# A three-layer transformer block: rotary pair swap on VectorE instead of TensorE, row sums and gates as column tiles of 32, halved TensorE steps, a new order of steps

## The reference

```python
x = x + xattn(layernorm(x), ctx, ctx, mask)   # scores without softmax, 16 heads of 16, then layernorm
x = x + attn(layernorm(x))                    # causal softmax attention, 16 heads of 16
x = x + ffn(layernorm(x))                     # rotary attention, rmsnorm, shared SwiGLU + 8 experts, rmsnorm
```

```python
r = jnp.stack([x1 * cos - x2 * sin, x1 * sin + x2 * cos], axis=-1)
q, k = src @ Wq, src @ Wk_c @ Wk              # both roped; v = src @ Wv_c @ Wv
g = softmax(flat @ Wg_gate + group_bias)      # 2 groups; the best group's 4 experts, top 2 of them
out = x + silu_glu(flat, W_shared_in) @ W_shared_out + sum_e w[:, e] * (h @ W2_experts[e])
```

## Time and profile before

| | |
|---|---|
| median of three runs | 241.22 us (241.12 to 241.95) |
| span of the profiled execution, its own time | 239.0 us, first to last instruction |
| TensorE busy | 228.0 us (95%) in 2304 matmuls |
| VectorE busy | 171.9 us (72%) |
| ScalarE busy | 121.4 us (51%) |
| POOL busy | 75.3 us (32%) |
| moved by DMA | 26.35 MB |
| first Gram matmul, last matmul's end | 6.0 us, 234.2 us |

### The profile page before, as it was taken

The page is one execution under the profiler, slowest core; times in us unless marked ns, Lnnn a source line. Parts: engine busy times, 40 slices in busy tenths (PEclk is TensorE's granted clock), DMA queues, the critical chain, the costliest instruction groups (busy, mean ns, idle before and its releaser), DMA issues.

```text
span 239.0 us, 5721 instructions
## 1 busy us (share of the span) xinstructions
PE 228.0 (95%) x2304; PEld 205.4 (86%) x2304; DVE 171.9 (72%) x370; ACT 121.4 (51%) x245; POOL 75.3 (32%) x89
## 2 busy tenths in 40 slices
PE   6989899999999999999999999999999999999991
PEld 6987797999999889978989999988878879998881
DVE  0757876966987879887966789586697764448353
ACT  3754575238571766386177977815451553550000
POOL 3011026222634020513549567745110020731011
PEclk9999999999999999999999999999999999999998
DMA  6899999828153452023304511100000000000001
GB/s 221 265 298 394 353 357 320 300 85 268 75 175 102 106 174 71 21 69 109 88 4 118 170 70 32 58 1 3 0 3 0 3 0 3 0 22 3 3 0 66
DMA packets 9434, 26.35 MB, mean 110 GB/s; under 512 B 1464, under 2 KB 2752, under 8 KB 9280
## 3 DMA queue, kind: packets, MB, share of 16 engines
q1 hardware_dynamic: 9120, 25.47, 32.4%
q10 hardware_dynamic: 288, 0.52, 0.6%
HBM read 25.46 MB, written 0.52 MB: 109 GB/s over the span
## 4 chain that ended last, share of the span: by engine, by line
PE 83%; DMA 7%; issue 3%; ACT 3%; DVE 2%; SPq 1%; POOLq 0%; POOL 0%; DVEq 0%
PE ps L704 77%; DMA raw<-in_ctx 7%; PE ps L707 5%; ACT ch L578 1%; DVE cl L1143 1%; ACT probT L511 1%; SPq L403 0%; DVE Z L1304 0%; SPq L358 0%; POOLq L363 0%; POOL rstd L463 0%; ACT z0T L511 0%; DVE X L1313 0%; DVE mb L1184 0%; DVE xHL L1273 0%
## 5 line engine op out<-in xcount | busy, mean ns | idle before, releaser
L704 PE MATMUL ps<-ch 128*128 128x130 f32 (+1 forms) x208 | 51.4, 264 | 1.5 <-DVE cl L1143 1.4
L704 PE MATMUL ps<-ch,cl 128*128 128x260 f32 (+1 forms) x208 | 51.1, 308 | 0.0
L704 PE MATMUL ps<-w,hT 128*128 128x512 f32 (+1 forms) x204 | 45.9, 382 | 0.0
L704 PEld LDWEIGHTS ps<-w,hT 128*128 128x128 f32 x204 | 36.4, 188 | 7.7 <-issue 0.7
L1143 DVE TENSOR_TENSOR cl<-raw,ch 128x1024 fp32r<-128x1024 f32 (+4 forms) x31 | 31.9, 1051 | 14.9 <-ACT ch L578 14.7
L704 PEld LDWEIGHTS ps<-ch 128*128 128x128 f32 (+1 forms) x208 | 39.5, 190 | 2.9 <-issue 1.4
L704 PEld LDWEIGHTS ps<-ch,cl 128*128 128x128 f32 (+1 forms) x208 | 39.2, 188 | 0.2
L463 POOL TENSOR_TENSOR rstd<-ve,half_exp 128x1 f32<-128x1 f32 (+1 forms) x22 | 13.8, 628 | 73.0 <-DVE ve L1022 72.9
L578 ACT ACTIVATE ch<-raw 128x1024 fp32r<-128x1024 f32 (+4 forms) x31 | 27.5, 916 | 12.9 <-DMA raw<-in_ctx 10.8
L704 PE MATMUL ps<-xHL,dense 128*128 128x256 f32 x192 | 24.3, 285 | 0.0
L704 PEld LDWEIGHTS ps<-xHL,dense 128*128 128x128 f32 x192 | 23.4, 192 | 0.2
(11 more groups left out here) (161 smaller groups left out, 417.7 us busy)
## 6 DMA issues: line engine op xcount, KB each, us to landing
raw<-in_ctx SPq DMA_DIRECT2D x22, 512.0 KB, 4.6
raw<-in_w SPq DMA_DIRECT2D x8, 512.0 KB, 3.8
stage<-in_dense SPq DMA_DIRECT2D x4, 512.0 KB, 5.9
w<-in_w SPq DMA_DIRECT2D x4, 256.0 KB, 6.9
w<-in_w SPq DMA_DIRECT2D x1, 1024.0 KB, 8.4
mask<-in_mask SPq DMA_DIRECT2D x1, 800.5 KB, 7.5
raw<-in_ctx SPq DMA_DIRECT2D x8, 65.0 KB
raw<-in_ctx ACTq DMA_DIRECT2D x2, 256.0 KB, 4.7
```

Of the source, the lines that this page charges most:

```text
L704: return pe.matmul(o, l, r, start=start, stop=stop, skip_group_check=not check)
```

## The change

The shuffle, the column tiles and the halves, cut to the lines that matter:

```diff
 # rotary: VectorE, step keys2 (rotate and roped are gone, also on POOL, ScalarE, TensorE)
-                    for swapped, (dst, by) in enumerate(((kcos, "cos"), (krot, "sin"))):
-                        last = dve.tensor_tensor(dst[i % 2][:, :, :], ...
-                    last.then_inc(own("k_parts", i), 1)
+                    both = ps[:, tile_bank(i):tile_bank(i) + 2, 0:D]
+                    link(dve.stream_shuffle(turned.rearrange("p b c n -> p b (c n)"), both, SWAP))
+                    dve.tensor_tensor(summed, both..., const("cos")..., ALU.mult).then_inc(own("qk_taken", i), 1)
+                    link(dve.tensor_tensor(turned, turned, const("sin")..., ALU.mult))
+                    dve.tensor_tensor(summed, summed, turned, ALU.add).then_inc(own("roped", i), 1)
 # rotary: TensorE, step keys2 (values2 has no TensorE part any more)
-                    for swapped in range(2):
-                        for ob in range(KC):
-                            last = mm(ps[:, tile_bank(i), swapped * D + ob * P:swapped * D + (ob + 1) * P],
-                                      wkv[0:P // 2, swapped, ob * P:(ob + 1) * P], kvcT[i % 2][0:P // 2, :], True, True)
+                    for ob in range(KC):
+                        last = mm(ps[:, tile_bank(i), ob * P:(ob + 1) * P], wkv[0:P // 2, ob * P:(ob + 1) * P],
+                                  kvcT[i % 2][0:P // 2, :], True, True)
+                        if ob == 0:
+                            mm(ps[:, tile_bank(i) + 1, D:2 * D], kvcT[i % 2][P // 2:P, :], wkv[P // 2:P, :], True, True)
 # rotary: ScalarE (no copy to qs; values2 waits for qk_taken; keys_roped writes qp and kblk)
-                    act.wait_ge(own("q2", i), i // 2 + 1)
-                    copy(qs[i % 2][:, :, :], ps[:, tile_bank(i) + 1, 0:D]...)
 # row sums, TensorE: from cross2_product to cross3; svn on VectorE and its product on POOL move along
-                                last = mm(ps[:, CROSS_B[0], jb * 2:(jb + 1) * 2], w0[:, 2, k, jb * P:(jb + 1) * P],
-                                          scol[:, k, i - 1:i + 1], k == 0, k == KC - 1)
+                                for r in range(P // PAIR):
+                                    mm(ps[r * PAIR:(r + 1) * PAIR, CROSS_B[0], jb * 2:(jb + 1) * 2],
+                                       w0[:, 2, k, jb * P + r * PAIR:jb * P + (r + 1) * PAIR], scol[:, k, i - 1:i + 1],
+                                       k == 0, k == KC - 1)
 # gates, TensorE
+                            for r in range(P // PAIR):
+                                mine = slice(r * PAIR, (r + 1) * PAIR)
+                                last = mm(ps[mine, tile_bank(1) + 1, t * 16:t * 16 + GRP + E],
+                                          xT[:, k, t * P + r * PAIR:t * P + (r + 1) * PAIR], gate[:, k, :], ...)
 # halves, TensorE: each pair is the old step cut in two
+                elif step in ("gram_rows", "gram"):
+                elif step in ("cross2_half", "cross2_product"):
+                elif step in ("hidden_half", "hidden_product"):
+                elif step in ("experts_half", "experts_product"):
```

More of the change, by code:

```diff
@@ L74, in constants @@
     return c
+SWAP = [lane ^ 1 for lane in range(32)]
 NU = 5 + 8
@@ L117, in second_half_steps @@
     return [
[L118 to L122, removed]
@@ L123, in second_half_steps @@
-        ("gram", 19), ("roped", 0), ("shares", (1, 0)), ("score_product", (0, 1)), ("split", 21), ("score", (0, 1)),
-        ("turn_p", (1, 0)), ("cross1", 5), ("piece", 3), ("exp", (0, 1)), ("gram", 20), ("values", (1, 0)),
-        ("evac", 6), ("cross2_product", 5), ("shares", (0, 1)), ("cross2", 5), ("project", (1, 0)),
-        ("turn_p", (0, 1)), ("norm2", 1), ("cross3", 5), ("norm2_end", 1), ("split", 22), ("values", (0, 1)),
-        ("cross4", 5), ("turn_z", (1, 1)), ("project", (0, 1)), ("split", 23), ("proj2_product", 1), ("rotate", 1),
@@ L128, in second_half_steps @@
-        ("square", 0), ("rms1", 0), ("roped", 1), ("keys2", 1), ("values2", 1), ("keys_roped", 1), ("rms1_end", 0),
-        ("cross1", 6), ("gram", 21), ("turn_x", 0), ("score_product", (1, 1)), ("piece", 4), ("xo_product", 2),
-        ("score", (1, 1)), ("xo", 2), ("exp", (1, 1)), ("cross2_product", 6), ("shares", (1, 1)), ("gram", 22),
-        ("gram", 23), ("cross2", 6), ("xo_end", 2), ("turn_p", (1, 1)), ("norm1", 2), ("evac", 7), ("cross3", 6),
[3 rows of a table removed]
-        ("values1", 2), ("turn_x", 1), ("cross4", 7), ("piece", 8), ("score_product", (2, 0)), ("score", (2, 0)),
@@ L156, in second_half_steps @@
-        ("experts", (1, 2)), ("experts", (1, 3)),
+        ("turn_z", (0, 1)), ("norm1", 1), ("cross2", 4), ("cross2_product", 4), ("gram_rows", 17), ("norm1_end", 1),
+        ("split", 18), ("split", 19), ("proj2_product", 0), ("gram", 17), ("evac", 5), ("turn_z", (1, 0)),
+        ("cross3", 4), ("keys2", 0), ("split", 20), ("proj1_product", 1), ("cross1", 5), ("queries", 1),
+        ("score", (1, 0)), ("score", (0, 1)), ("shares", (1, 0)), ("shares", (0, 1)), ("keys1", 1), ("values1", 1),
@@ new lines, in second_half_steps @@
+        ("split", 23), ("square", 0), ("gram_rows", 21), ("rms1_end", 0), ("turn_z", (1, 1)), ("cross4", 5),
+        ("cross1", 6), ("proj2_product", 1), ("turn_x", 0), ("keys2", 1), ("cross2_half", 6), ("cross2_product", 6),
+        ("xo_product", 2), ("gram", 21), ("gram_rows", 22), ("values2", 1), ("xo", 2), ("xo_end", 2),
+        ("score_product", (1, 1)), ("gram", 22), ("gram_rows", 23), ("gram", 23), ("keys_roped", 1), ("norm1", 2),
+        ("score", (1, 1)), ("cross2", 6), ("norm1_end", 2), ("cross3", 6), ("shares", (1, 1)), ("exp", (1, 1)),
@@ L481, in _ @@
                     last.then_inc(sem("gpre"), 1)
-                elif step == "cross2" and i % 2:
+                elif step == "cross3" and i % 2:
                     t = i // 2
@@ L791, in _ @@
                         pe.wait_ge(sem("mb"), i)
+                    if i > 1 and i % 2 == 0:
+                        pe.wait_ge(sem("svn"), i // 2)
                     bank = ps[:, CROSS_B[0], :]
```

298 lines of the change are left out of this document (145 added, 153 removed), and 6 rows, old and new, of the table USES.

## The result

The changed kernel takes 248.2 us (248.0 to 248.8) against 241.2: a ratio of 1.028, with a 95% interval of [1.026, 1.031]. A fourth execution took 253.4 us at a granted clock of 0.966, where the others had 0.985 to 0.993, and such slower executions are left out of every time and ratio here. The kernel is slower by 7.0 us, and lies 12.6 us above the forecast of 235.6 and outside the range. Its profiled execution has a span of 246.2 us.

A forecast was written before the change was run, and what follows sets the result against it. The prediction took the kernel as TensorE-bound from 6 to 234 us and summed -4.1 - 2.0 - 1.0 + 0.8 - 1.8 + 2.5 = -5.6 us, 241.22 to 235.6 us, range 230.8 to 239.6 (the forecast's own 232.5 to 238.5).

The forecast's parts named there:

- (b): Row sums `sv` on TensorE: column tiles of 32 in place of full-width products, four calls, -2.0 us.
- (c): Gates on TensorE in column tiles of 32, 0.95 us to 0.46, twice: -1.0 us.
- the slow rival: Rotary shuffle on VectorE is dear: from 2.3 us each it eats the 5.6 us gain; chance 0.07.
- (a): Rotary pair swap moved from TensorE to a VectorE shuffle: -4.1 us, bounds a gain of 3.6 to 4.6.
- (d): Larger steps halved: more re-entries of fp32r blocks behind fp32 steps on TensorE, +0.8 us (0 to 1.7).
- (f): New order behind the opening: old waits go, -1.6, new short hand-offs cost +4.1; together +2.5 us, bounds -1.6 and +5.
- (e): New order in the opening: TensorE's waits for the first Gram block and z0T shrink, -1.8 us, at most 2.9.
- The third rival: VectorE sets the pace up to 130 us, so only the part behind gains: 0.0 in all, 241.2 us; chance 0.14.
- the sign that I had set for being wrong: TensorE's idle time between 44 and 130 us grows by more than 5 us, or the shuffle takes over 1.5 us.

The follow-up runs named there:

- kernel with eight pieces placed: Changed kernel with eight of POOL's weight-piece steps moved, some behind waits, all work done, VectorE's and TensorE's order kept: 241.51 us, 1.000 of the kernel before.
- kernel with memsets: Changed kernel with POOL's weight-piece subtractions replaced by fills with zero, leaving out the dense weights' low halves: 239.8 us, 0.994 of the kernel before.

## Why the prediction was wrong

**Right.** (b) and (c): 128 row-sum records in 1.9 us and 64 gate records in 0.9, -2.9 us of TensorE for the -3.0 forecast. The shuffle 0.73 us for 0.69, so the slow rival's condition (2.3 us) was not met. (a) to (d) together as a size: in the kernel with eight pieces placed TensorE is busy 222.4 us in all, 5.6 less than before, for a forecast of -7.1 + 0.8. Its parts were not right one by one. By starts, the rotary part of the four tiles went from 8.1 us to 2.6, so (a) gained 5.5 where its bounds were 3.6 to 4.6; the new step takes 0.64 us, not 0.9, in the changed kernel's TensorE timeline:
```profile
178.35 0.37 PE L706 MATMUL ps<-kvcT,wkv 64*128 64x128 f32 x1 [0.37 <-ACT kvcT L517]
...
178.99 3.01 PE L706 MATMUL ps<-w,hT 128*128 128x512 f32 x12
```
So the rest of TensorE's work grew by some 3 us where (d) had 0.8, and what made it grow no run shows. Of the short hand-offs in (f), `turn_x 1` cost 0.95 us in the changed kernel, `cross1 7` 0.64, the kvcT copies 0.6, for forecasts of 1.3, 0.5 and 0.9; tile 1's rope (0.8) cost nothing.

**The step that failed is (f)**, "I added up TensorE's work between each step and the one that needs its result through other engines". That sum gives each VectorE instruction the length it had in the trace before. But the new order also puts pieces on POOL right behind the roots of `xo 3` and of `norm2` of tiles 2 and 3, and there POOL's next instruction holds the very instruction that POOL has just released; other pieces meet the shares. The forecast had nothing for it. Placing the pieces took 6.7 us off, leaving the subtractions out 8.4. I had the evidence: the 2366 ns in the earlier trace rows. I took it as a bound for the shuffle and asked only how it compared with the median, not what ran beside it. Two more lines of the trace before answer that:
```profile
127.18 2.36 POOL L498 TENSOR_TENSOR w<-raw,w 128x1024 fp32r<-128x1024 f32 x1
```
```profile
127.45 2.37 DVE L1050 SCALAR_TENSOR_TENSOR Z<-Z,rstd,rows 128x256 f32<-128x256 f32 x1
```
POOL was named in the prediction as "neither is the bound", and of moved POOL steps I had counted the roots, not what stands behind a root in its queue.

**The second failure is the size of (e) and (f) with most of the holds gone.** 235.6 was forecast; with the pieces placed it is 241.5. TensorE's waits listed in that kernel sum to 12.0 us, against 6.0 before (1.0 of each at the start, for the blank tile): +6.0 where (e) and (f) together had +0.7. The places named in (f) were about right; those that I had not named (0.9 us at `turn_x 0` is one) are the rest, and some of them are holds that remain. Its largest:
```profile
PE ps L687 <- DVE cl L1134: 2.7, 3, 1.3
PE ps L690 <- DVE prob L1223: 1.5, 2, 1.3
...
PE ps L687 <- ACT kblk L510: 1.3, 1, 1.3
```
Two of these waits stand behind held instructions. VectorE and POOL of this kernel:
```profile
30.51 2.39 POOL L458 TENSOR_TENSOR X<-X,rows 128x1024 f32<-128x1024 f32 x1 [5.31 <-DMA rows<-in_rows]
...
31.26 2.99 DVE L1134 TENSOR_TENSOR cl<-raw,ch 128x1280 fp32r<-128x1280 f32 x1 [1.48 <-ACT ch L565]
...
167.46 4.69 POOL L485 TENSOR_TENSOR w<-raw,w 128x1024 fp32r<-128x1024 f32 x2 [0.59 <-DVE Z L1029]
...
170.23 2.47 DVE L1242 TENSOR_TENSOR swapped<-swapped,cst 128x512 f32<-128x512 f32 x1
```
A chunk's low half, 1.48 us at its shortest, takes 2.99 beside POOL's addition to X, and TensorE waits 1.2 us for it at 34.4 us; the sine product of tile 2's rope takes 2.47 us in place of 0.68 beside a piece, and the wait on `kblk` follows. So the step that failed in (f) took part in (e) too, which said that Gram rows would cover the low halves. Behind the first data, the largest wait that is no hold is 1.3 us, for tile 0's shares. `cl` was also TensorE's largest wait on results in the kernel before, and the five that I read there leave it out:
```profile
PE ps L704 <- DVE cl L1143: 1.4, 2, 0.9
```
How much (e) gained is not settled: TensorE got to `xo_product 0` 0.9 us earlier in the changed kernel, and 0.4 to 1.9 us earlier in the ten others that keep its opening, for a forecast of 1.8; the new opening on the old order lost. The third rival, VectorE setting the pace, was the nearest in kind; it looked up to 130 us, and most of the loss lies behind. So did the sign that I had set for being wrong: between 44 and 130 us TensorE's idle time grew by 3.3 us, not by 5.

What stays open: what the shuffle is worth in the new order, since the run for it had waits of its own; what the kernel would take with no hold at all; and why one gap of 2.1 us was followed by the lower clock and two longer ones were not.

## What to carry to other kernels

When an order is changed, list for each engine what stands directly behind the instruction that releases another engine: if it is a long POOL instruction on SBUF data, the released VectorE instruction may wait for all of it, so put it behind a wait for that instruction or where VectorE reads PSUM or reduces. A duration in the trace that is five times its group's median is a question, what ran beside it, before it is a bound. And TensorE work that is saved counts only up to the next chain that it covered: 7 us less work in the old order moved the end by nothing.

## What the runs showed of the hardware

A 128x256 normalise of 0.41 us took 2.46 beside a 128x1024 POOL subtraction of 2.38, and in the kernel with memsets one took 1.90 beside POOL instructions that only write; a 0.72-us POOL quarter grew in turn. With one operand in PSUM (0.48 us) and in a reduction (1.22 us) nothing was added. A gap of 2.1 us in TensorE's work (161.7 to 163.8) was followed by most of 4 us at 1.2 GHz, and behind one of 4.1 us some 5 us of work ran at it: these two late results cost 1.7 and some 2.7 us beyond their own length. Gaps of 2.7 and 2.3 us in the changed kernel were followed by no lower clock.
